# TensorE's code for eight experts: a loop over pairs against a program written out in full

## The reference, cut to what matters

```python
logits = einsum('th,eh->te', h, router_weight)            # 4096 tokens, 8 experts
topk_probs, selected = top_k(softmax(logits), 2)
capacity = ceil(1.25 * 4096 * 2 / 8)                      # 1280 slots for each expert
expert_inputs = zeros((8 * capacity + 1, 256)).at[dispatch].set(h[st])
pre  = einsum('ech,edh->ecd', expert_inputs, ff_pre_act_weight)      # 256 -> 1024
gate = einsum('ech,edh->ecd', expert_inputs, gate_weight)            # 256 -> 1024
expert_out = einsum('ecd,ehd->ech', pre * silu(gate), ff_post_act_weight)  # 1024 -> 256
out = zeros((4096, 256)).at[st].add(expert_out[dispatch] * kept_w)
x = layernorm(x + out)
```

## Time and profile before

| | |
|---|---|
| time, median of 3 runs | 1847.5 us (1847.24 to 1848.12) |
| span of the profiled execution, first to last instruction | 1837.5 us |
| own time of the profiled execution | not given beside its span; the median of the runs is 10.0 us above the span |
| PE (TensorE's matmuls) busy | 1655.9 us, 90% of the span |
| PEld (TensorE's weight loads) busy | 1015.6 us, 55% |
| DVE (VectorE) busy | 1170.0 us, 64% |
| ACT (ScalarE) busy | 1287.7 us, 70% |
| POOL (GpSimd) busy | 296.5 us, 16% |
| mean granted TensorE clock | 0.966 |

### The profile page before, as it was taken

The page is one execution under the profiler, slowest core; times in us unless marked ns, Lnnn a source line. Parts: engine busy times, 40 slices in busy tenths (PEclk is TensorE's granted clock), DMA queues, the critical chain, the costliest instruction groups (busy, mean ns, idle before and its releaser), DMA issues. The chain is left out here.

```text
span 1837.5 us, 31725 instructions
## 1 busy us (share of the span) xinstructions
PE 1655.9 (90%) x10818; PEld 1015.6 (55%) x10819; DVE 1170.0 (64%) x2192; ACT 1287.7 (70%) x1485; POOL 296.5 (16%) x296
## 2 busy tenths in 40 slices
PE   7939999999999999999999976499989999999995
PEld 6713333333333333333333333488978987889985
DVE  6847767686868686867787766635445443545474
ACT  7739999999999999999999985334233242432333
POOL 0000000000000000000000010144332514434153
PEclk9969999999999999999999998799989999999998
DMA  5562101001010101010101006023231313323043
GB/s 162 190 159 68 36 20 33 23 29 26 26 26 26 29 23 31 20 33 19 34 18 35 17 23 228 13 61 74 50 80 39 106 39 77 75 53 104 11 126 114
DMA packets 74747, 108.27 MB, mean 59 GB/s; under 512 B 10778, under 2 KB 59715, under 8 KB 74672
## 3 DMA queue, kind: packets, MB, share of 16 engines
q1 hardware_dynamic: 59792, 89.42, 15.7%
q0 software_dynamic: 14880, 17.82, 5.6%
HBM read 75.77 MB, written 35.91 MB: 61 GB/s over the span
## 5 line engine op out<-in xcount | busy, mean ns | idle before, releaser
L690 ACT ACTIVATE probs<-scores 128x1536 f32<-128x1536 f32 (+1 forms) x384 | 520.7, 1379 | 42.9 <-PE scores L620 37.6
L620 PE MATMUL scores<-aq,ak 98*128 98x512 bf16 (+3 forms) x1280 | 303.5, 352 | 57.9 <-DMA aq<-shift_dram 23.0
L733 DVE TENSOR_REDUCE sums<-expq 128x1 f32<-128x1408 f32 (+6 forms) x448 | 347.4, 828 | 13.0 <-ACT expq L696 13.0
L636 PE MATMUL o_ps<-probs,vh 128*32 128x512 f32 (+3 forms) x2560 | 339.0, 541 | 0.0
L1367 ACT ACTIVATE gate<-up_ps 128x512 f32<-128x512 f32 x128 | 76.5, 598 | 331.2 <-PE up_ps L1194 331.2
L620 PE MATMUL scores<-ak,aq 98*128 98x512 bf16 (+3 forms) x1184 | 263.7, 342 | 17.1 <-ACT probs L690 9.0
L696 ACT ACTIVATE expq<-scores 128x1536 f32<-128x1536 f32 x192 | 274.7, 1449 | 1.9
L620 PEld LDWEIGHTS scores<-aq,ak 98*128 98x128 bf16 x1280 | 96.5, 98 | 230.5 <-ACT probs L690 73.2
L720 DVE TENSOR_TENSOR hidden<-probs,after 128x384 f32<-128x384 f32 x128 | 70.9, 554 | 239.6 <-ACT probs L690 239.6
L620 PEld LDWEIGHTS scores<-ak,aq 98*128 98x128 bf16 x1184 | 91.0, 98 | 238.4 <-ACT expq L696 94.7
L1194 PE MATMUL up_ps<-xeT_hi,wup_hi 128*128 128x512 f32 x512 | 204.3, 399 | 18.3 <-issue 13.2
(11 more groups left out here) (238 smaller groups left out, 2569.1 us busy)
## 6 DMA issues: line engine op xcount, KB each, us to landing
raw<-w_T SPq DMA_DIRECT2D x16, 1024.0 KB, 7.7
split_dram<-parts SPq DMA_DIRECT2D x48, 256.0 KB, 2.9
aq<-split_dram SPq DMA_DIRECT2D x192, 64.0 KB
raw<-wg_T SPq DMA_DIRECT2D x8, 1024.0 KB, 4.9
ak<-split_dram SPq DMA_DIRECT2D x32, 192.0 KB
xT<-x_T SPq DMA_DIRECT2D x8, 512.0 KB, 4.6
ak<-split_dram SPq DMA_DIRECT2D x32, 128.0 KB
x_sb<-x_tok SPq DMA_DIRECT2D x1, 4096.0 KB, 26.4
```

The costliest lines, as they stand in the source:

```text
L620: last = nc.tensor.matmul(dst[:, at:at + w], still, moving[0:KS, lo:lo + w], start=True, stop=True, skip_group_check=True)
L636: last = nc.tensor.matmul(dst[32 * r:32 * r + 32, BLK - w:BLK], vh[j % 2][:, k, :], probs[:, m % P_RING, at:at + w], start=first, stop=Tru ...
L690: last = nc.scalar.activation(probs[:, m % P_RING, 0:w], src[:, 0:w], ACT.Exp, scale=HD ** -0.5)
L733: last = nc.vector.tensor_reduce(sums[:, j % 2, col:col + 1], expq[:, n % X_RING, at:at + w], AX.X, ALU.add)
```

## The change

TensorE gets another driver. It calls the same `body` eight times in a row with constant numbers; expert 7 is still the one with `prep` false. No loop is left around TensorE's experts. ScalarE, VectorE, GpSimd and SyncE keep `experts`.

```diff
+            def experts_in_full(eng, body):
+
+                for e in range(E):
+                    body(e // 2, e % 2, e < E - 1)
+
             def extra(eng, i, j):
 
                 e = i * 2 + j
...
-                experts(pe, body)
+                experts_in_full(pe, body)
```

## The result

The changed kernel takes 1823.4 us (median of 4 runs, 1821.83 to 1823.7). The kernel before, on the same chip, takes 1847.4 us (4 runs, 1845.2 to 1848.12). The ratio is 0.987 (95% interval 0.9857 to 0.9882): 24.0 us less. The forecast was 1829.9 us, 17.6 us less, with a range from 1827.5 to 1834.6.

The account below looks back on a forecast made before the run. TensorE was taken to bound the kernel, stalled by its loop's two jumps back. Gaps 11.96 + slow clock 5.66 + 0 = 17.6 us off the 1837.5 span gives 1819.9; plus 10.0 makes 1829.9 us, range 1827.5 to 1834.6.

Parts of the forecast that it names:

- the last of the sum: Outside the profiled span: the median's 10.0 us above it stays, turning the forecast span of 1819.9 into 1829.9 us.
- The two gaps: TensorE's idle pieces before experts 2 and 4, from jumping back: 6.03 and 5.93 us, 11.96 us gained.
- The slow clock behind them: First 48 matmuls of experts 2 and 4 return from 14.10 and 13.34 to 10.89 us: 5.66 us gained.
- The forward branches: Skips at L1216: one dear in five as before, taken as 0; bounds 1.58 us gain, 4.7 us loss.
- Straight code must be fetched: TensorE's about six bodies in place of two: fetching costs nothing; 7.6 us if all six new borders exposed it.
- The other engines' loops: The other engines keep their loops at 0.06 us a jump, hidden beside TensorE's matmuls; 0.1 us if uncovered.
- The end moves as a block: All after expert 6 hangs on TensorE and GpSimd's adds and moves forward together; expert 7 begins at 1727.6.
- The queueing behind SyncE's loads: Two 1 MB transfers just before a jump back make it some 2.8 us dearer than the worst forward branch.
- A: Rival: the gaps close but TensorE's slow stretch has another cause; only 11.96 us gained, 1835.5 us; chance 0.05.
- C: Rival: the jump is cheap and something that stays holds TensorE's sequencer; no change, 1847.5 us; chance 0.04.
- D: Rival: the longer TensorE program is loaded within the measured time; slower, 1891 us; chance 0.02.
- B: Rival: skips or page borders of the long program become dear at more places; 1834.6 or 1842.2 us; chance 0.07.

Follow-up runs that it names:

- experiment 1: Both kernels run again with no edit and spans listed: the kernel before took 1844.4 us, the changed kernel 1821.6 us.
- again_before: The kernel before run again with no edit, for spans and a second profile: 1844.4 us (10 runs), ratio 1.0002; profiled span 1842.6.
- late_gather_before: The kernel before with GpSimd's gather of the next expert's tokens held back until the first half's eight up products are done: ratio 0.9996.
- one_jump: The kernel before with TensorE's experts 0 and 1 written out and experts 2 to 5 left in the loop: 1830.4 us, ratio 0.9930.
- norest_short_loop: The kernel before, rows past the first 1024 of experts 1, 3, 6 left out, the rest's code removed from TensorE's loop: 1793.1 us, ratio 0.9708.
- late_load: The kernel before with SyncE's load of the next up weights held back until TensorE's first up product of the current expert: 1836.7 us, ratio 0.9963.
- again_after: The changed kernel run again with no edit, for a second profile: 1821.6 us, ratio 0.9885 to the kernel before.
- late_load_after: The changed kernel with SyncE's load of the next up weights held back until the current expert's first up product: 1820.2 us, ratio 0.9897 to before.
- shifted_after: The changed kernel with some 115 repeated waits just ahead of TensorE's first transposition of the experts: 1824.4 us, ratio 0.9919 to the kernel before.
- padded_after: The changed kernel with some 113 instructions of repeated waits before TensorE's branch over the second round of routing: 1826.0 us, ratio 0.9929 to before.
- all_full: The changed kernel with the programs of all five engines written out, no loop over experts left: 1820.2 us, ratio 0.9894 to the kernel before.
- under 8: Comparison of profiles, no new kernel: in expert 7 TensorE's wait for `mid` is split in the changed kernel; clock behind it 1.00 against 0.91, 1.57 us.
- before_look: The kernel before run once more with no edit, for another profile: time 1841.25 us, span 1839.4.

## Why the prediction was wrong

**The step that failed** is the last of the sum: "The median is 10.0 us above the span, and I leave that as it is". It was a constant without a reason, and the range gave it no width of its own. Only 1.7 to 1.9 us lie around the span in the runs that list both (2.05 in one). The other 8.2 us were executions of the kernel before that last longer than the profiled one. Such time can belong to the very thing that the change removes, and most of it went with the change: the four spans of the changed kernel lie within 1.4 us below and 0.5 above its profiled one. With 1.8 in place of 10.0 the same sum gives 1819.9 + 1.8 = 1821.7, against 1823.4 measured. What else was off by a term adds 1.6 to 1.7: in spans, 17.6 forecast and 16.0 measured. The mechanism was right, and this one term was mis-sized.

**Where the 8.2 us come from.** The profiled execution of before is shorter than all its timed ones: its own time would be some 1839.3, beside runs of 1845.2 to 1848.1. Two things can do that, and which it was is open, since the chip of that profile is not on record. It may have been a quick execution, though none of the 24 spans of experiment 1 is as short. Or it ran on a quicker chip: the kernel before took 1837.8 and 1839.5 us on two chips, and 1843.8, 1846.3 and 1847.4 in the three other sets of runs. The changed kernel or its neutral variants took 1820.1, 1820.2, 1821.6 and 1823.4 in four of these five. So before differs by 9.6 us and after by 3.3, and the gain is 18 us on one chip and 24 on another. What makes before long on some chips goes with the loop, and the sum, read from one quick profile, is right where such executions are the rule (17.7 and 19.3 us).

**Where in the program it lies** is shown in part. again_before is 5.1 us longer than the first profile, and has it in expert 4, behind the second jump, which is 5.5 us longer: 0.8 more gap, 0.7 more slow matmuls, and the stop for `mid` with its own slow stretch, some 4 us. Its expert 0 is 2.0 us longer, and shorter pieces elsewhere make up for that. late_gather_before has the long second branch too (7.08 us, gap 6.79). Stops for `mid` inside experts 2 and 4 appear in three profiles, all with a dear jump just before (again_before 2.1 us, one_jump 0.6, norest_short_loop 1.0 and 0.5), and in none without one. That the jump causes them was not tested. Late answers also occur in expert 0, where there is no jump, but TensorE has also just stood still.

The spread of the executions is a weaker sign. On the chip of experiment 1 the spans reach over 7.4 us in the kernel before (24 runs), 4.1 with one jump (4 runs), 1.8 in late_load (5) and 1.7 in again_after (4); without a rest over 10.0 and 5.9 with dear jumps, 2.3 with cheap ones and 1.1 with none (4 each). But late_load_after, shifted_after and padded_after have no jump and reach over 4.9, 3.9 and 4.5 us (5 runs each). A dear jump is not the only thing that varies.

**Point by point.**

- *The two gaps, 11.96 us:* right. Both are gone, and nothing took their place at the borders.
- *The slow clock behind them, 5.66 us:* right. 10.95 us for 48 matmuls at both places, 0.06 above the 10.89 that was taken. Expert 2 gained 9.20, forecast 9.24.
- *The forward branches, 0:* off by 0.5 us in the sum, and wrong in its places. Expert 5 gained its 1.58 and expert 4 lost 1.07 (69.04 against 67.97). Three of the five skips were affected, not one. Expert 2's took 1.6 us, covered by queued matmuls. Expert 7's took 3.6 us, under the wait for `mid`. In expert 4 the branch itself was short (338 ns), and the stop came one matmul later, when the next piece was not there. The count by the 256 instructions to a page that the Trainium skill gives ("Advanced Engine Details and Errata", section "ISA Cache") named expert 4 for the gap, which the trace bears out. It also said that no other branch would be long, which the trace contradicts for experts 2 and 7. The count can be put right after the fact: leave the labels that branches aim at out of it, and set one border by where TensorE stopped in expert 4. Then expert 4's branch lands 2 instructions before the end of a piece, expert 7's leaps over a whole piece (3.6 us), expert 2's stands 25 instructions behind the start of one (1.6 us) and expert 5's 48 (0.42 us). With the same border, the branch of expert 0 lands 3 instructions before the end of a piece in shifted_after and 5 in padded_after, where TensorE stopped behind one matmul and two. No kernel was run to test this count ahead of its result.
- *Straight code must be fetched, 0:* right but for that one gap of expert 4. Six new bodies, no gap at a border.
- *The other engines' loops, 0:* right (all_full).
- *The end moves as a block:* wrong by 1.56 us, in the kernel's favour, for the reason under 8.
- *Expert 0, which the prediction did not name:* 3.81 us more, so that expert 7 began at 1730.80 and not at 1727.6. The 69.60 of the first profile is the lowest of all: 71.63 in again_before, 70.68 in before_look, up to 76.3 in the other kernels with a loop, and 69.7 to 73.5 in those without. These overlap, so nothing shows that the change has a part in it.
- *The queueing behind SyncE's loads, 2.8 us for a jump:* right (late_load: 2.4 and 2.8 less gap than in the first profile, 2.4 and 3.7 less than on the same chip).

Of the rivals, A (the clock does not come back), C (nothing) and D (slower) did not happen. B's moved gap is the 1.07 us of expert 4 and no more; of the signs that were to prove the forecast wrong, that gap is the only one that appeared.

## What to carry to other kernels

Before a sum is made against a profile, ask what the profiled execution's own time is. If the median is higher, look for what varies between executions and between chips; do not book it as a constant. Here a loop on TensorE was cheap or dear by its length and its place. When its branch shows microseconds in the sequencer's rows, shorten the body, shift it, or write it out. A jump like this one cost 8 to 14 us in these profiles (6 to 7 of standing still, 2 to 3 at the lower clock and, in some executions, more behind it). Count the padding's own time before you shift code: 115 instructions of waits took 12.5 us. The two loads of 1 MB issued just before such a jump added some 3 us to it, and moving them gave 7.1 of the 22 us that writing the loop out gave on that chip.

## What the runs showed of the hardware

- A branch on TensorE had four prices here: 0.07 to 0.50 us to code at hand, 0.9 to 1.6 us in expert 2 of the kernels written out and not padded, probably for a piece already on its way, 3.3 to 3.8 us to code not at hand, and 6.0 to 7.1 us for the same with 2 MB of transfers ahead of it.
- A loop of 1668 instructions jumped back in 0.21 us, or in 6.0 to 6.5, by where it lay.
- A wait of TensorE of 3.3 us in one piece cost 1.6 us more behind it, at a granted clock of 0.91, than one of 1.4 and 1.7 us with 24 matmuls between them, at 1.00.
- ScalarE can take up a product microseconds after TensorE's last matmul of it: 3.5 us in expert 0 of the changed kernel (1208.2 to 1211.7) and 3.5 us in expert 4 of again_before (1538.4 to 1541.8). This was seen up to some 20 us after TensorE had stood still, and not everywhere there. Holding back the gathers did not change the time of the kernel before (ratio 0.9996). Its cause is open.
